# Second attention: who turns the weight tiles of the next head group

## The reference, cut to what matters

```python
def _L0_cond2_ref(x, Wq, Wk, Wv, Wo, q_norm_w, k_norm_w, k_cache, v_cache, block_table, cache_seqlens):
    q = jnp.einsum('bsd,ed->bse', x, Wq).reshape(bsz, seqlen, HQ, D)      # HQ 32, D 128
    k = jnp.einsum('bsd,ed->bse', x, Wk).reshape(bsz, seqlen, HK, D)      # HK 8
    v = jnp.einsum('bsd,ed->bse', x, Wv).reshape(bsz, seqlen, HK, D)
    q = _rope(_rmsnorm(q, q_norm_w), pos); k = _rope(_rmsnorm(k, k_norm_w), pos)
    k_all = jnp.concatenate([k_cache[block_table].reshape(bsz, 512, HK, D), k], axis=1)
    v_all = jnp.concatenate([v_cache[block_table].reshape(bsz, 512, HK, D), v], axis=1)
    scores = jnp.einsum('bqhd,bkhd->bhqk', q, k_all) * SCALE              # 4 query heads per key head
    o = jnp.einsum('bhqk,bkhd->bqhd', softmax(where(valid, scores)), v_all)
    return jnp.einsum('bse,de->bsd', o.reshape(bsz, seqlen, HQ * D), Wo)
```

## Time and profile before

| what | value |
|---|---|
| median of 3 runs | 1540.57 us (1540.3 to 1542.01) |
| the profiled execution's own time | 1550.29 us |
| span of its profile | 1548.6 us, TensorE clock granted 0.989 of full |
| steps of the second attention | from 320.6 us to some 1480 us of the span |

### The profile page before, as it was taken

How to read it: one execution, slowest core, us unless ns; L and a number is a source line. 1 busy time by engine, 2 the same in 40 slices (tenths; PEclk the granted TensorE clock), 3 DMA queues, 4 the chain that set the end, 5 groups by cost and what they waited for, 6 DMA issues and landing times.

```text
span 1548.6 us, 26991 instructions
## 1 busy us (share of the span) xinstructions
PE 1485.0 (96%) x8792; PEld 1269.1 (82%) x8792; DVE 1208.1 (78%) x2700; ACT 866.8 (56%) x2260; POOL 878.9 (57%) x1231
## 2 busy tenths in 40 slices
PE   6699999989999999999999999999999999999997
PEld 4588888778888888888888888888888888888885
DVE  5688887778778887788788888878788888777865
ACT  2322232356666666666666666666666666666641
POOL 1111343256666666766676676667666766676521
PEclk9899999999999999999999999999999999999999
DMA  8988765222212221222122222212221222211102
GB/s 184 230 169 173 171 137 148 80 83 72 79 55 71 69 77 57 72 68 71 57 81 71 69 68 75 71 55 73 80 69 57 74 74 59 88 57 50 41 27 82
DMA packets 169701, 133.37 MB, mean 86 GB/s; under 512 B 119187, under 2 KB 128787, under 8 KB 169563
## 3 DMA queue, kind: packets, MB, share of 16 engines
q1 hardware_dynamic: 152098, 97.56, 23.9%
q0 software_dynamic: 16464, 33.85, 7.4%
q10 hardware_dynamic: 1000, 0.23, 0.1%
HBM read 107.47 MB, written 7.34 MB: 74 GB/s over the span
## 4 chain that ended last, share of the span: by engine, by line
PE 86%; SPq 5%; ACT 2%; issue 2%; DVE 2%; POOL 1%; DMA 1%; POOLq 0%; DVEq 0%
PE ps_t L932 14%; PE ps_o L746 11%; PE ps_o L748 11%; PE ps_o L747 10%; PE ps_b L746 5%; PE ps_b L748 5%; PE ps_b L747 5%; PE ps_q L748 4%; PE ps_q L747 4%; PE ps_q L746 4%; PE ps_a L746 3%; PE ps_a L747 3%; PE ps_a L748 3%; SPq L454 2%; PE ps_a L795 2%
## 5 line engine op out<-in xcount | busy, mean ns | idle before, releaser
L1418 ACT ACTIVATE sm<-sm,mn 128x640 f32<-128x640 f32 x256 | 211.4, 826 | 233.6 <-DVE mn L1908 227.1
L1784 DVE TENSOR_TENSOR pT_lo<-ps_t,pT_hi 128x512 fp32r<-128x512 f32 x320 | 220.2, 688 | 114.5 <-ACT pT_hi L1341 101.5
L629 POOL DMA_INDIRECT kraw<-in_L_cond_k_cache_dram,idx_a x200 | 197.4, 987 | 89.2 <-issue 75.7
L1341 ACT ACTIVATE pT_hi<-ps_t 128x512 fp32r<-128x512 f32 x320 | 188.5, 589 | 85.1 <-PE ps_t L932 82.2
L629 POOL DMA_INDIRECT vraw<-in_L_cond_v_cache_dram,idx_a x200 | 198.6, 993 | 59.6 <-issue 59.3
L932 PE MATMUL ps_t<-ident,sm 128*128 128x128 f32 x1280 | 196.4, 276 | 3.5 <-DVE sm L1920 1.5
L932 PEld LDWEIGHTS ps_t<-ident,sm 128*128 128x128 f32 x1280 | 148.7, 141 | 51.6 <-DVE qT_lo L1784 17.5
L646 POOL TENSOR_TENSOR z<-pairs_p,zl 128x128 f32<-128x128 f32 x160 | 57.9, 402 | 193.6 <-DVE pairs_p L1637 193.6
L746 PE MATMUL ps_o<-wo_lo,oT_hi 128*128 128x512 f32 x256 | 118.0, 461 | 12.4 <-ACT kvown L1345 10.8
L746 PE MATMUL ps_o<-pT_lo,v_hi 128*128 128x512 f32 x320 | 129.8, 405 | 0.0
L748 PE MATMUL ps_o<-pT_hi,v_hi 128*128 128x512 f32 x320 | 125.5, 392 | 0.0
(11 more groups left out here) (257 smaller groups left out, 4305.6 us busy)
## 6 DMA issues: line engine op xcount, KB each, us to landing
fv<-st SPq DMA_DIRECT2D x128, 128.0 KB, 2.4
tab<-tab_scratch SPq DMA_DIRECT2D x64, 256.0 KB
wblk<-n_L_attn_weight_qkv_dram SPq DMA_DIRECT2D x32, 384.0 KB
wpraw<-_L_attn_weight_proj_dram SPq DMA_DIRECT2D x8, 1024.0 KB, 5.6
mask<-mask_scratch SPq DMA_DIRECT2D x64, 128.0 KB
wtile<-in_L_cond_Wq_dram SPq DMA_DIRECT2D x28, 256.0 KB
wtile<-in_L_cond_Wo_dram SPq DMA_DIRECT2D x28, 256.0 KB
kraw<-in_L_cond_k_cache_dram,idx_a POOLq DMA_INDIRECT x200
```

The source lines that it names most:

```text
L629: pool.indirect_dma_start(raw[:, par, c, :], None, rows_d, bass.IndirectOffsetOnAxis(idx[:, k:k + 1].bitcast(U32), 0)).then_inc(arrived[pa ...
L1341: act.activation(dst, src, ACT.Copy).then_inc(t_hi, 1)
L1418: act.activation(sm[:, h, :], sm[:, h, :], ACT.Exp, bias=mn[:, h:h + 1], scale=-1.0, accum_out=den[:, h:h + 1]).then_inc(e_done, 1)
L1784: dve.tensor_tensor(lo, src, hi.bitcast(F32), ALU.subtract).then_inc(t_lo, 1)
```

## The change

1. Tiles are loaded in pieces of 32 floats (128 bytes), by four DMAs of 32 partitions each, such that turning each 32 x 32 block by itself gives the whole tile turned. VectorE turns a tile in one instruction (`turn`) from `wtile` into the place where its low part will stand (`wa_turn` and `wo_turn` are other names for the memory of `wa_lo` and `wo_lo`).
2. ScalarE makes the high part from there (`turned_hi`) behind group D0, and the low part is a subtraction in place: GpSimd's for the first tile of a step, ahead of stats_k, VectorE's for the second, at the step's end.
3. The steps now have 1, 1, 1, 1, 1, 1, 2, 2 tiles. The W groups are gone from TensorE and from `ps_t`.
4. TensorE waits for `wt_lo_pool` and `wt_lo_dve` before it uses the next head's weights, and SyncE loads a tile's successor when it is turned.
5. The hidden features of Wo stand in another order (feature f at 128 (f mod 4) + f // 4); the last layer's weights are transposed with columns 4 apart to match, and four copies of head 0's Wo tiles read PSUM at that step. These lines are left out below.

```diff
@@ -333,17 +339,20 @@
 
-        W_FIRST = {0: 0, 1: 1, 2: 3, 3: 4, 4: 6, 5: 7, 6: 9}
-        W_COUNT = {0: 1, 1: 2, 2: 1, 3: 2, 4: 1, 5: 2, 6: 1, 7: 0}
+        W_FIRST = {0: 0, 1: 1, 2: 2, 3: 3, 4: 4, 5: 5, 6: 6, 7: 8}
+        W_COUNT = {0: 1, 1: 1, 2: 1, 3: 1, 4: 1, 5: 1, 6: 2, 7: 2}
         PRO = HG + 2
 
         def groups_of(n, last):
+            w = []
             if last:
                 w = [f"L{i}" for i in range(7) if i // 2 + 1 == n] + [f"Y{i}" for i in range(2) if N - 2 + i == n]
-            else:
-                w = [f"W{W_FIRST[n] + i}" for i in range(W_COUNT[n])] if W_COUNT[n] else []
             nxt = not (last and n == N - 1)
             return w + ["K"] * nxt + ["D0", "D1", "D2"] + ["q"] * nxt + ["D3", "DS"]
+
+        def tiles_of(n, last):
+
+            return [W_FIRST[n] + i for i in range(W_COUNT[n])] if W_COUNT[n] and not last else []
 
...
@@ -405,7 +414,7 @@
                 return wa[:, one, :, t * P:(t + 1) * P].rearrange("p a c m -> p (a c) m")
-            return wo_t[:, one, :, (t - 6) * P:(t - 5) * P].rearrange("p a h m -> p (a h) m")
+            return wo_t[:, one, :, :].rearrange("p a h (j q b) -> p (a h) q j b", j=4, q=4)[:, :, t - 6, :, :]
 
...
@@ -484,7 +493,13 @@
                     src = wo[(t - 6) * P:(t - 5) * P, bass.ds(g * QW, QW)]
-                sp.dma_start(wtile[:, slot, :], src).then_inc(wt_in[slot], 16)
+                if t < 6:
+                    blocks = src.rearrange("(j b) (c i a) -> i b c j a", j=4, c=NC_, i=4)
+                else:
+                    blocks = src.rearrange("(b j) (c i a) -> i b j c a", j=4, c=NC_, i=4)
+                for i in range(4):
+                    sp.dma_start(wtile[32 * i:32 * i + 32, slot, :].rearrange("b (u v a) -> b u v a", u=4, v=4),
+                                 blocks[i]).then_inc(wt_in[slot], 16)
 
...
@@ -535,14 +550,12 @@
                     load_wtile(g + 1, 1, 1)
-                for name in groups_of(n, last):
-                    if name[0] == "W" and int(name[1:]) + 2 < TILES_W:
-                        t = int(name[1:])
-                        wait_alone(sp, t_full, base + t_index(n, name, last)[0] + 1)
+                for t in tiles_of(n, last):
+                    if t + 2 < TILES_W:
+                        wait_alone(sp, wt_turned, g * TILES_W + t + 1)
                         load_wtile(g + 1, t + 2, t % 2)
-                    elif name[0] == "W" and g + 2 < G:
-                        t = int(name[1:])
-                        wait_alone(sp, t_full, base + t_index(n, name, last)[0] + 1)
+                    elif g + 2 < G:
+                        wait_alone(sp, wt_turned, g * TILES_W + t + 1)
                         load_wtile(g + 2, t + 2 - TILES_W, t % 2)
...
@@ -701,6 +714,11 @@
                     gather(v_rows, vraw, vg_in, idx, (n + 2) % N, par, range(KC - 1))
+                for t in tiles_of(n, last)[:1]:
+                    wait_alone(pool, wt_hi, g * TILES_W + t + 1)
+                    pool.tensor_tensor(w_dst(wa_lo, wo_lo, (g + 1) % 2, t), w_dst(wa_turn, wo_turn, (g + 1) % 2, t),
+                                       w_dst(wa_hi, wo_hi, (g + 1) % 2, t).bitcast(F32),
+                                       ALU.subtract).then_inc(wt_lo_pool, 1)
                 if not (last and n == N - 1):
...
@@ -1104,7 +1115,7 @@
                     if n == N - 1:
-                        pe.wait_ge(t_lo, base + t_index(6, "W9", last)[0] + 1 + 2)
+                        pe.wait_ge(wt_lo_pool, g * N + 6)
                     project_q(n1, wpar1, [0, 1])
...
@@ -1126,6 +1137,9 @@
                         pe.wait_ge(kv_copied, J + 2)
+                    if g >= 1 and n == 1:
+                        pe.wait_ge(wt_lo_pool, g * N)
+                        pe.wait_ge(wt_lo_dve, g * 2)
                     out_proj(wpar0, [0])
...
@@ -1387,6 +1403,12 @@
 
+            def turned_hi(g, t):
+
+                act.wait_ge(wt_turned, g * TILES_W + t + 1)
+                act.activation(w_dst(wa_hi, wo_hi, (g + 1) % 2, t),
+                               w_dst(wa_turn, wo_turn, (g + 1) % 2, t), ACT.Copy).then_inc(wt_hi, 1)
+
             def late_copy(idx, bank, i):
...
@@ -1440,6 +1463,8 @@
                 group("D0")
+                if tiles:
+                    turned_hi(g, tiles[0])
                 exponentials(2)
...
@@ -1457,6 +1482,8 @@
                 group("D3")
+                if len(tiles) > 1:
+                    turned_hi(g, tiles[1])
                 if nxt:
...
@@ -1881,7 +1910,18 @@
                 nxt = not (last and n == N - 1)
-                w = [m for m in names if m[0] in "WLY"]
+                w = [m for m in names if m[0] in "LY"]
+                tiles = tiles_of(n, last)
+
+                def turn(t):
+
+                    dve.wait_ge(wt_in[t % 2], (g * (TILES_W // 2) + t // 2 + 1) * 64)
+                    raw = wtile[:, t % 2, :]
+                    if t < 6:
+                        raw = raw.rearrange("p (c m) -> p c m", c=NC_)
+                    else:
+                        raw = raw.rearrange("p (j c a) -> p c j a", j=4, c=NC_)
+                    dve.transpose(w_dst(wa_turn, wo_turn, (g + 1) % 2, t), raw).then_inc(wt_turned, 1)
 
...
@@ -1929,10 +1969,14 @@
                     group(w[1])
+                if tiles:
+                    turn(tiles[0])
                 if not (first and n < 1):
                     output_lo(J)
                 if nxt:
                     group("K")
+                if len(tiles) > 1:
+                    turn(tiles[1])
                 group("D0")
...
@@ -1956,6 +2000,12 @@
                 group("DS")
+                if len(tiles) > 1:
+                    t = tiles[1]
+                    dve.wait_ge(wt_hi, g * TILES_W + t + 1)
+                    dve.tensor_tensor(w_dst(wa_lo, wo_lo, (g + 1) % 2, t), w_dst(wa_turn, wo_turn, (g + 1) % 2, t),
+                                      w_dst(wa_hi, wo_hi, (g + 1) % 2, t).bitcast(F32),
+                                      ALU.subtract).then_inc(wt_lo_dve, 1)
                 if first and n == 2:
```

More of the change, by code:

```diff
@@ L132, in block_program @@
         wa_lo = at("wa_lo", [P, 2, NC_, PW], F32R, 160)
+        wa_turn = at("wa_turn", [P, 2, NC_, PW], F32, 160)
+        wo_turn = at("wo_turn", [P, 2, HG, HID], F32, 64)
         wtile = at("wtile", [P, 2, HID], F32, 184)
@@ L266, in block_program @@
         wt_in = [sem(f"wt_in{i}") for i in range(2)]
+        wt_turned = sem("wt_turned")
+        wt_hi = sem("wt_hi")
+        wt_lo_pool = sem("wt_lo_pool")
+        wt_lo_dve = sem("wt_lo_dve")
         tab_in = [sem(f"tab_in{i}") for i in range(2)]
@@ L423, in hi_lo_target @@
                 return pT[:, 0:KC, h * P:(h + 1) * P], HID
-            return w_dst((wa_hi, wa_lo)[lo], (wo_hi, wo_lo)[lo], (g + 1) % 2, int(name[1:])), HID
+            raise KeyError(name)
         def late_parts(bank, i, lo):
@@ L933, in transposed @@
                 return mm.then_inc(t_full, 1)
-            def w_tile(idx, bank, t, arrivals):
-                pe.wait_ge(wt_in[t % 2], arrivals)
-                transposed(idx, bank, [(c, wtile[:, t % 2, c * P:(c + 1) * P]) for c in range(NC_)])
             def k_group(idx, bank, g, n):
@@ L1033, in late_group @@
                 if t < NC_:
-                    transposed(i, bank, [(c, wbraw[:, t, c * P:(c + 1) * P]) for c in range(NC_)])
+                    transposed(i, bank, [(c, wbraw[:, t, c:HID:NC_]) for c in range(NC_)])
                 elif t == 4:
-                    transposed(i, bank, [(c, earaw[:, c * P:(c + 1) * P]) for c in range(NC_)])
+                    transposed(i, bank, [(c, earaw[:, c:HID:NC_]) for c in range(NC_)])
                 elif t == 5:
@@ L1039, in late_group @@
                     for c in range(NC_):
-                        mm = pe.transpose(ps_t[bank][:, c * P:c * P + E], gateraw[:, c * P:(c + 1) * P],
+                        mm = pe.transpose(ps_t[bank][:, c * P:c * P + E], gateraw[:, c:HID:NC_],
                                           ident[0:E, 0:E])
@@ L1340, in copy_hi @@
                     src = src.rearrange("p (c m) -> p c m", c=dst.shape[1])
+                if len(dst.shape) == 4:
+                    src = src.rearrange("p (h b j) -> p h j b", h=HG, j=4)
                 act.activation(dst, src, ACT.Copy).then_inc(t_hi, 1)
@@ L1783, in copy_lo @@
                     src = src.rearrange("p (c m) -> p c m", c=hi.shape[1])
+                if len(hi.shape) == 4:
+                    src = src.rearrange("p (h b j) -> p h j b", h=HG, j=4)
                 dve.tensor_tensor(lo, src, hi.bitcast(F32), ALU.subtract).then_inc(t_lo, 1)
```

3 lines of the change are left out of this document (removed).

## The result

The change makes the kernel **slower**, by 0.6%: 1549.16 us (1547.18 to 1552.1, 5 runs) against 1540.3 us (1535.82 to 1542.01, 5 runs) for the kernel before beside it, a ratio of 1.0057 with a 95% interval of 1.0038 to 1.0075. The forecast was 1527 us and faster, with a range from 1510 to 1541 us; the measured time lies above it.

A forecast was written before the change was run, and what follows sets the result against it. TensorE's own work was taken to set the step, with GpSimd's 1.26 us of idle time ahead of `ms` as second bound. 1550.3 - 30.8 + 10.0 + 6.0 + 1.4 = 1536.9, less 9.7: 1527 us, range 1510 to 1541.

The forecast's parts named there:

- W groups leave TensorE: -30.8 us: On TensorE, 70 transpose groups disappear at 0.44 us each, leaving steps of 17.58 us: -30.8 us.
- GpSimd's subtraction: +10.0 us: Ahead of the key's statistics, GpSimd's 1.30 us subtraction makes `ms` 0.20 us late in 50 steps: +10.0 us.
- Step 0: +6.0 us: In step 0 of heads 1 to 6, moved row indices leave the subtraction no cover: 6 by 1.0 us.
- Second tiles, turn, high part, DMA: +1.4 and nothing: Second tiles in steps 6 and 7 cost 7 by 0.2 us; VectorE's turn, ScalarE's high part and small-piece loads cost nothing.
- The profiled execution: -9.7 us: The profiled execution stands 9.7 us above the runs' median, before and after the change, so 1536.9 becomes 1527 us.
- the 17.4 I had: Losses in the sum: +10.0 for GpSimd's subtraction, +6.0 for step 0, +1.4 for second tiles.
- GpSimd as the bound: Rival: GpSimd's loop sets the step if its subtraction exceeds 2.20 us; up to 1553 us, chance 0.10.
- distances of 17.6 to 18.0 us: Sign of being right: time between TensorE's group K of steps 1 to 7 is 17.6 to 18.0 us.
- group DS waiting for `qT_lo`: Sign of being right: TensorE's group DS waits for VectorE's low part of q, and that for `rs`.

The follow-up runs named there:

- experiment 5: Changed kernel with GpSimd's subtraction moved between the cached values' low part and the first gather of values; 1527.28 us, 0.9905 of the kernel before.
- experiment 10: Changed kernel with GpSimd's subtraction ahead of the first value gather and tiles spread 0, 1, 1, 1, 1, 2, 2, 2; 1522.08 us, 0.9814 of the kernel before.
- experiment 9: Changed kernel with GpSimd copying the turned tile (one SBUF operand) at the same place instead of subtracting; 1571.61 us, 1.0128 of the kernel before.
- experiment 11: Changed kernel again, no edit, one execution in another session; 1579.56 us against 1549.74 for the kernel before.
- experiment 2: Changed kernel with GpSimd's subtraction moved from ahead of the key's statistics to behind the statistics of q; 1532.55 us, 0.9942 of the kernel before.

## Why the prediction was wrong

*W groups leave TensorE: -30.8 us.* Right. Where nothing else is late a step takes 17.59 us (experiments 5 and 10), the 17.58 of the earlier trace rows.

*GpSimd's subtraction: +10.0 us.* **This is the step that failed**, in its direction and in its size. It took rows 7 to say that two instructions can hold each other up, gave the delay to GpSimd and priced it as `ms` late by 0.20 us. The runs show the reverse: the piece keeps its length (1.28 to 1.32 us), `ms` still waits for ScalarE in 28 of the 35 steps numbered 2 to 6, and VectorE's rotary sum is held until GpSimd is done. I had read the start of the piece from step 7, where the third gather ends 7.91 us after K, and took the sum, 0.29 us ahead of that, to be the first and therefore the winner. Rows 7 had already spoken against that, as the prediction itself says: VectorE's normalise began 0.02 us first, and it was the one held up. In half of the steps of the kernel after the gather ends at 7.36, so the piece is first (in 29 of the 45 overlaps); and in the 16 where the sum is first, it loses all the same. In steps 1 to 7 it is TensorE's group q that waits, for the sum (27.2 us in 46 times), and not group DS for a late `rs`. The price of the place is 0.45 us in the five plain steps, 1.0 us in step 1 and 0.8 us in step 7 (steps of 18.59 and 18.42 against 17.58): 4.1 us a head, 28.7 us in seven, against the 10.0 of the sum. The Trainium skill ("SBUF — State Buffer", Who interferes with whom) says of such a pair that whoever issues first gets the port and the other is blocked in full. For the subtraction with its two operands a full block is borne out; that the first wins is not what the rows show, by the starts that the profile gives, since VectorE lost with a lead of up to 0.63 us. The copy of experiment 9 does not agree with a full block: where the sum began first, both were lengthened. The Trainium skill says elsewhere ("GPSIMD Engine Reference", Elementwise — side-by-side cycle accounting) that such a subtraction takes about twice VectorE's time: 1.29 against 0.68 here, agreed.

*Step 0: +6.0 us.* The mechanism is right (in step 0 `ms` waits for the piece and starts 10.53 us after K), the size too small: the step takes 18.93 us, 1.35 above 17.58, or 9.4 us in 7 heads. The sum took the moving of the row indices as covered, as it was in the longer steps before. It is not: without a tile in step 0 the step takes 18.15 us (experiment 10), so 0.56 us of the excess is the row indices and only the rest the piece: 0.8 us here, 1.0 with the piece early (19.14).

*Second tiles, turn, high part, DMA: +1.4 and nothing.* Right, within the 1.4. The turn takes 0.70 us (I took 0.68), the high part 0.62, both behind other work; with the sum out of the way, steps with two tiles take 17.59 us. The small pieces cost about 1.5 us.

*The profiled execution: -9.7 us.* Right as a correction: a second trace of the kernel before has 9 us less of late copies. But such waits can also come with the change: in the one execution of experiment 11 there are 51.8 us of late copies, and the time is 30 us more. That was not among my rivals.

Summed again with what the rows show: a head loses 5 x 0.45 + 1.35 + 1.01 + 0.84 = 5.45 us, 38.2 us in seven, in place of the 17.4 I had; 1550.3 - 30.8 + 38.2 - 9.7 = 1548.0, against 1549.2 measured. The medians leave out single long steps, which stand in both traces, so a fit this close is partly luck. The rival that I had for slower, GpSimd as the bound, did not happen either: GpSimd idles 0.5 us in front of `ms` in a plain step, and with the same load the step is 17.65 us in experiment 2. To name distances of 17.6 to 18.0 us as a sign of being right was too weak a test; group DS waiting for `qT_lo` was the sharper one, and it waits 2.5 us in all.

## What to carry to other kernels

Before moving an instruction with SBUF operands to GpSimd, lay VectorE's timeline beside the new place and look for instructions with two SBUF operands. For a GpSimd instruction that also reads two, take it that VectorE waits until it is done, whoever starts first, and price what waits for VectorE. With the same instruction in four places the kernel was 3.7% slower, 0.6% slower, 0.6% faster or 0.9% faster than before; beside a product with one operand in PSUM it cost nothing. When every step gets shorter, look again at work that was only just covered: the row indices had 0.08 us to spare before, and cost 0.56 us a head afterwards. And read more than one step: the step that looks most like the future (no W group) had a gather timing that few others had.

## What the runs showed of the hardware

- A VectorE instruction reading two operands from SBUF ends 0.55 to 0.57 us (a 512-column sum) after an overlapping GpSimd subtraction, in 45 of 45 rows in each of two traces; a VectorE lead of up to 0.63 us does not help (16 rows in the one, 39 in the other). A short GpSimd instruction behind it can be held in turn: `ms` took 0.5 us instead of 0.19 in 15 steps of the kernel after.
- GpSimd writing only (0.54 us) costs VectorE's sum nothing (0.68 us in 43 of 43 overlaps). GpSimd reading one operand lengthens both when VectorE began first (43 rows), VectorE from 0.68 to 0.82-0.88 us in most and itself from 0.62 to about 1.0.
- VectorE's product with one operand in PSUM keeps its 0.69 us beside GpSimd's subtraction (47 rows of experiment 5).
- The signal of a finished group of matmuls can reach all who wait for it late by the timeline: ScalarE started 0.2 to 1.67 us after the matmuls' modelled end instead of 0.04, in none of 56 steps of one trace of the kernel after and in 44 of 56 of the other, from another session. The row shows it as ScalarE waiting for TensorE; why it happens stays open.
